# One memory map for three stages of a float32 image kernel: buffers of the next stage filled in the tail of the last, the turn between them in halves, transform rows and five tiles kept in SBUF

## What is computed

```python
xn = layernorm(groupnorm(x))                       # 64 channels
left  = (xn @ left_w  + b) * mask * sigmoid(xn @ lgate_w + b)
right = (xn @ right_w + b) * mask * sigmoid(xn @ rgate_w + b)
out = einsum('bkjd,bkid->bijd', left, right)       # 512x512x512 in each of 64 channels
out = (layernorm(out) @ out_w + out_b) * sigmoid(xn @ ogate_w + b)
x = x + out                                        # layer 0; the result is "x1" below
f = fft2(groupnorm(x))[:12, :12]                   # 12 x 12 modes of each channel
x = x + real(ifft2(f mixed by a complex 64x64 weight in each mode))   # layer 1
```

## Time and profile before

| | |
|---|---|
| device time, median of 3 runs | 3049.51 us (3048.06 to 3056.5) |
| the profiled execution, time | 3050.38 us |
| the profiled execution, span | 3048.6 us |
| mean granted PE clock | 0.950 of full speed |
| PE, DVE, ACT, POOL busy | 83%, 72%, 45%, 33% of the span |
| moved by DMA | 950.26 MB, 312 GB/s over the span |

### The profile page before, as it was taken

How to read it: one execution, slowest core, us unless ns; L and a number is a source line. 1 busy time by engine, 2 the same in 40 slices (tenths; PEclk the granted TensorE clock), 3 DMA queues, 4 the chain that set the end, 5 groups by cost and what they waited for, 6 DMA issues and landing times. The chain is left out here.

```text
span 3048.6 us, 40917 instructions
## 1 busy us (share of the span) xinstructions
PE 2516.1 (83%) x12694; PEld 1875.4 (62%) x12694; DVE 2203.9 (72%) x3463; ACT 1373.3 (45%) x1778; POOL 1021.2 (33%) x1042
## 2 busy tenths in 40 slices
PE   0008999989989979999999993889898899789785
PEld 0005666656666648888888882556565666588664
DVE  5997888778778848898888986667676676326443
ACT  0007888778778866677666672112122122100000
POOL 1018888778778820000000000344444444300000
PEclk9999999999999989999999996899999999769998
DMA  9845888887878766777777773999999999849999
GB/s 375 341 182 203 316 318 313 305 309 287 301 298 297 289 269 254 283 287 276 278 281 282 288 276 103 381 373 382 379 386 366 376 389 374 266 162 382 419 419 406
DMA packets 260650, 950.26 MB, mean 312 GB/s; under 512 B 31153, under 2 KB 31665, under 8 KB 260146
## 3 DMA queue, kind: packets, MB, share of 16 engines
q1 hardware_dynamic: 226160, 877.25, 76.2%
q10 hardware_dynamic: 34370, 71.54, 6.1%
HBM read 540.83 MB, written 407.90 MB: 311 GB/s over the span
## 5 line engine op out<-in xcount | busy, mean ns | idle before, releaser
L652 DVE SCALAR_TENSOR_TENSOR pj_lr<-pj_v_ps,layer_b_val,pj_sig 128x1024 f32<-128x1024 f32 x256 | 328.7, 1284 | 163.2 <-ACT pj_sig L589 162.7
L1104 POOL TENSOR_TENSOR fi_square_sum<-fi_square_sum,fi_square 128x1024 f32<-128x1024 f32 x128 | 302.8, 2366 | 424.7 <-ACT fi_square L1075 424.7
L780 PE MATMUL ct_acc_ps<-ct_l_hi,ct_r_hi 128*128 128x512 f32 x1024 | 406.2, 397 | 20.6 <-ACT ct_l_hi L794 20.6
L781 PE MATMUL ct_acc_ps<-ct_l_lo,ct_r_hi 128*128 128x512 f32 x1024 | 405.9, 396 | 0.0
L782 PE MATMUL ct_acc_ps<-ct_l_hi,ct_r_lo 128*128 128x512 f32 x1024 | 405.9, 396 | 0.0
L1075 ACT ACTIVATE fi_square<-fi_x 128x1024 f32<-128x1024 f32 x128 | 135.4, 1058 | 596.0 <-DVE fi_x L1132 583.9
L490 POOL TENSOR_TENSOR front_ring<-front_ring,layer_gn_shift 128x512 f32<-128x512 f32 x256 | 331.2, 1295 | 40.3 <-DVE front_ring L618 40.3
L1031 PE MATMUL fi_y_ps<-fi_scaled,layer_w_bd 128*128 128x512 f32 x512 | 280.7, 631 | 65.5 <-DVE fi_scaled L1115 65.4
L1115 DVE TENSOR_TENSOR fi_scaled<-fi_m,fi_s_ps 128x512 f32<-128x512 f32 x256 | 174.3, 681 | 191.0 <-DMA fi_m<-mixed_d 166.0
L589 ACT ACTIVATE pj_sig<-pj_g_ps,layer_b_gate 128x1024 f32<-128x1024 f32 x256 | 285.6, 1116 | 42.6 <-PE pj_g_ps L555 37.4
L1302 PE MATMUL la_ps_ps<-la_col,la_inv_cols 128*128 128x256 f32 x1024 | 242.9, 400 | 50.1 <-DVE la_early L1372 28.5
(11 more groups left out here) (183 smaller groups left out, 4979.9 us busy)
## 6 DMA issues: line engine op xcount, KB each, us to landing
lr_d<-pj_lr SPq DMA_DIRECT2D x128, 1024.0 KB, 5.4
gate_d<-pj_gout SPq DMA_DIRECT2D x128, 512.0 KB, 6.8
ct_l<-lr_d SPq DMA_DIRECT2D x64, 1024.0 KB, 7.0
ct_r<-lr_d SPq DMA_DIRECT2D x64, 1024.0 KB, 9.0
mixed_d<-ct_o SPq DMA_DIRECT2D x64, 1024.0 KB, 5.0
fi_m<-mixed_d SPq DMA_DIRECT2D x128, 512.0 KB, 14.2
fi_g<-gate_d SPq DMA_DIRECT2D x128, 512.0 KB, 13.3
fi_x<-in_x SPq DMA_DIRECT2D x32, 2048.0 KB, 9.4
```

Source lines behind the costliest of these rows:

```text
L652: dve.scalar_tensor_tensor(out=out[:, :, RG * (m % 2):RG * (m % 2) + RG], in0=v_ps[:, :].rearrange("p (q i) -> p q i", i=RG), scalar=keep. ...
L780: pe.matmul(bank, high, l_hi[b][:, :, k, :], start=(k == 0), stop=False)
L781: pe.matmul(bank, high, l_lo[b][:, :, k, :], start=False, stop=False)
L1104: pool.tensor_tensor(square_sum[:, :, :], square_sum[:, :, :], square[:, :, :], ALU.add).then_inc(sum_done, 1)
```

## The change

- **One area.** The SBUF tiles of `contract`, `finish_layer0` and `layer1` lie at fixed places of one tile `area` (a new class `Shared`), and the matrices that only the front needs are given back after `project`. So SP can fill buffers of `finish_layer0` during the last channel of `contract`.
- **Filled early.** At the last channel SP issues the loads of four gate chunks and x tiles 0 to 3, then the last store of `mixed_d`, then x tile 4; after the stores of `mixed_d` have landed, four mixed chunks.
- **The turn.** Mean squared is taken on ACT. One multiplication by a mask made beforehand on POOL takes the place of two. From there on the chain works in two halves (e = 0, 1) of 128x1024. The high part goes by four DMAs of a half straight from SBUF to its place in `st` on ACT's queue, the low part on SP's; `scale_d` is gone.
- **`finish_layer0`.** Its slots are written out for SP, ACT, POOL and DVE too (PE's were). The x ring has five tiles. The transform has two PSUM banks. Its four small DMAs go into one SBUF tile `rows` (one partition each, runs of 1 KB) and come ahead of the x1 store; the last five x1 tiles are not stored but stay where they are.
- **`layer1`.** No load of the rows. The ring has eight buffers, five of them hold the kept tiles, which are worked on first; one load comes after the column transform, two after the inverse over the rows, the others as stores free their buffers. Stores to `out` are issued by ACT, loads by SP.

```diff
+class Shared:
+    def __init__(self, t, x, mixed_d, gate_d):
+        self.xt = [self.at("fi", f"x{b}", 16 * b, [TG, WS, C]) for b in range(XT)]      # XT = 5
+        self.mt = [self.at("fi", f"m{b}", 80 + 4 * b, [GW]) for b in range(MB)]         # MB = 4
+        self.gt = [self.at("fi", f"g{b}", 96 + 4 * b, [GW]) for b in range(MB)]
+        self.rows = self.at("fi", "rows", 112, [M2, TG * C])
+        self.st = self.at("fi", "s", 136, [RG, GW], F32R)
...
 def contract(nc, lr_d, mixed_d, keep, mid):
...
+        def spread_part(eng, part, source, e):
+            for q in range(RG):
+                rows = slice(P // 4 * q, P // 4 * q + P // 4)
+                at = P // 2 * part + P // 4 * e
+                eng.dma_start(mid.st[at:at + P // 4, q, :].bitcast(F32),
+                              source[rows, e, :, :].rearrange("p t j -> p (t j)").bitcast(F32)).then_inc(mid.s_loaded, DMA)
...
+                if isinstance(n, int) and n == C - 1:
+                    for c in range(MB):
+                        mid.load_gate(sp, c)
+                    sp.wait_ge(l_low, C)
+                    sp.wait_ge(r_low, C)
+                    for k in range(2):
+                        mid.load_x(sp, k)
+                    sp.wait_ge(summed, WT * (C - 1))
+                    for k in range(2, 4):
+                        mid.load_x(sp, k)
                 sp.wait_ge(out_dve, n + 1)
                 sp.wait_ge(out_act, 3 * n + 3)
                 sp.dma_start(view[2][n], flat(om[b])).then_inc(stored[b], DMA)
 
             channels(sp, body)
-            sp.wait_ge(scale_split, 2)
-            for k in range(2):
-                sp.dma_start(scale_v[k], flat((r_hi, r_lo)[k][0]).bitcast(F32)).then_inc(scale_stored, DMA)
-            sp.wait_ge(scale_stored, 2 * DMA)
+            sp.wait_ge(summed, WT * C)
+            for k in range(4, XT):
+                mid.load_x(sp, k)
             for b in range(2):
                 sp.wait_ge(stored[b], DMA * (C // 2))
+            for c in range(MB):
+                mid.load_mixed(sp, c)
+            for e in range(2):
+                sp.wait_ge(low_ready, e + 1)
+                spread_part(sp, 1, s_low, e)
...
+            act.activation(mean_sq[:, :, :, :], total[:, :, :, :], ACT.Square, scale=1.0 / C).then_inc(mean_squared, 1)
+            for e in range(2):
+                act.wait_ge(root_in, e + 1)
+                act.activation(total_sq[:, e, :, :], total_sq[:, e, :, :], ACT.Sqrt, bias=keep.eps[:, 0:1]).then_inc(root_ready, 1)
+            for e in range(2):
+                act.wait_ge(scale_ready, e + 1)
+                act.activation(s_high[:, e, :, :], total[:, e, :, :], ACT.Copy).then_inc(high_ready, 1)
+                act.wait_ge(high_ready, e + 1)
+                spread_part(act, 0, s_high, e)
...
+            for e in range(2):
+                dve.wait_ge(root_ready, e + 1)
+                link(dve.reciprocal(total[:, e, :, :], total_sq[:, e, :, :]))
+                dve.tensor_tensor(total[:, e, :, :], total[:, e, :, :], keep.mask_row[:, e, :, :],
+                                  ALU.mult).then_inc(scale_ready, 1)
+            for e in range(2):
+                dve.wait_ge(high_ready, e + 1)
+                dve.tensor_tensor(s_low[:, e, :, :], total[:, e, :, :], s_high[:, e, :, :], ALU.subtract).then_inc(low_ready, 1)
...
 def finish_layer0(nc, x1_d, keep, mid):
...
+                k = n // TH + 3
+                if n % TH == 4 and XT <= k < TILES:
+                    sp.wait_ge(x1_stored[k % XT], DMA * (k // XT))
+                    mid.load_x(sp, k)
...
                 if piece == 0:
                     pe.wait_ge(x1_ready, TG * k + TG)
-                    at_least(pe, f_copied, k)
+                    at_least(pe, f_copied, k - 1)
...
-                    act.dma_start(x1_v[k], xt[tile][:, :, :, :].rearrange("p g t c -> p g (t c)")).then_inc(x1_stored[tile], DMA)
                     for r in range(RG):
-                        act.dma_start(f_v[k, r], four[b][M2 * r:M2 * r + M2, :, :]).then_inc(f_stored[b], DMA)
+                        act.dma_start(mid.rows[RG * k + r:RG * k + r + 1, :, :], four[b][M2 * r:M2 * r + M2, :, :]).then_inc(
+                            f_stored[b], DMA)
+                    if k < KEPT:                                                      # 27
+                        act.dma_start(x1_v[k], xt[k % XT].rearrange("p g t c -> p g (t c)")).then_inc(x1_stored[k % XT], DMA)
...
 def layer1(nc, x1_d, w_real, w_imag, inverse_rows, inverse_columns, out, keep, mid):
...
+    XR = XT + 3
+    TILE = [(KEPT + n) % NTG for n in range(NTG)]
...
-            sp.dma_start(early[:, 0:M2 * WT * C], fourier_d.rearrange("p m r c -> p (m r c)")).then_inc(f_loaded, DMA)
...
+            sp.wait_ge(f_ready, 1)
+            load(XT)
+            sp.wait_ge(col_ready, C // CB)
+            for n in range(XT + 1, XR):
+                load(n)
+            for n in range(XR, NTG):
+                sp.wait_ge(stored[n % XR], DMA * (n // XR))
+                load(n)
...
+            for n in range(NTG):
+                act.wait_ge(y_done, WS // 2 * n + WS // 2)
+                act.dma_start(o_v[TILE[n]], by_group(xt[n % XR])).then_inc(stored[n % XR], DMA)
```

More of the change, by code:

```diff
@@ L975, in at_least, with halves, inside @@
+        block = ctx.enter_context(nc.Block())
+        def halves(lead, slot):
+            for n in range(-lead, HALVES + 2 * TH + 4):
+                slot(n)
+        def inside(n, count=HALVES):
+            return 0 <= n < count
         def at_least(eng, sem, value):
-            if not (is_int(value) and value <= 0):
+            if value > 0:
                 eng.wait_ge(sem, value)
-        def part(m, j, ahead, size):
-            return (LOOP // size) * j + (m + ahead) // size
         @block.sync
@@ L1010, in slot @@
                     sp.wait_ge(y_gated, n + 1)
-                    load_gate(c + MR, m // 2 % MR)
-                if m % TH == 4 and ahead_of(n, 2 * TH, HALVES):
-                    k = part(m, j, 2 * TH, TH)
-                    b = (m // TH + 2) % XR
-                    if not (is_int(k) and k < XR):
-                        sp.wait_ge(x1_stored[b], DMA * part(m, j, 2 * TH, LOOP))
-                    load_x(k, b)
-            halves(sp, 0, slot)
+                    mid.load_gate(sp, c)
@@ L1091, in _ @@
+            halves(0, slot)
+            for b in range(XT):
+                act.wait_ge(x1_stored[b], DMA * len(range(b, KEPT, XT)))
             for b in range(2):
-                act.wait_ge(f_stored[b], RG * DMA * (GROUPS // TG // 2))
+                act.wait_ge(f_stored[b], RG * DMA * (TILES // 2))
         @block.gpsimd
@@ L1097, in _, with slot @@
             pool.wait_ge(sum_set, 1)
-            def slot(n, m, j):
-                if m % 2 == 1 and ahead_of(n, -3, HALVES):
-                    g = part(m, j, -3, 2)
+            def slot(n):
+                if n % 2 == 1 and inside(n - 3):
+                    g = n // 2 - 1
                     pool.wait_ge(squared, g + 1)
@@ L1144, in _ @@
+            halves(2, slot)
             link = chained(dve, step)
```

395 lines of the change are left out of this document (184 added, 211 removed).

## The result

| | before | after |
|---|---|---|
| median of the runs, us | 3049.59 (3046.72 to 3056.5, n = 8) | 3065.61 (3059.31 to 3076.67, n = 8) |
| profiled execution: time, span | 3050.4, 3048.6 | 3064.27, 3062.5 |
| ratio of the times | | 1.0055 (1.0042 to 1.0068) |

The kernel became 16 us slower, 0.55%, where 60 us less were forecast. The interval is clear of 1, so the change is real, though small. The parts before and behind `finish_layer0`'s steady loop came out close to the forecast, and the loop took back more than all of them.

A forecast was written before the change was run, and what follows sets the result against it. DMA traffic and its waits were taken to set finish_layer0's pace, with little moving at the turn and layer1's start. 3050.4 - 17.7 - 3.3 - 8 - 17.2 - 14.5 = 2989.7, so 2990 us; range 2955 to 3025.

The forecast's parts named there:

- Step 3: finish_layer0's steady loop, halves 20 to 255: 648.0 us against 652.1, plus 4 for full buffers, 8 us less.
- I take 0.5 us, near the low end: Loop: cost a tile of four small DMAs into neighbouring partitions, between 0.24 and 7.6 us; cancels 0.55 saved.
- That costs nothing while SP's queue still holds loads, as it does then: Loop: small DMAs ahead of the x1 store start it some 1.9 us later, at no cost.
- The order that makes the loop stays: Loop: slot 4 still waits for a store issued two slots earlier, so 22.43 us a tile stays the base.
- another 4: Loop start: full buffers at half 20 give two tiles at 20.7 us before the DMAs are behind, 4 us less.
- Rival B: Loop longer through single-partition row DMAs: over 2.3 us a tile, chance 0.05; 1 to 2.3 us, 3016 to 3050, chance 0.12.
- Step 1: Turn from contract to finish_layer0: 17.7 us less, first matmul of the finish at 1892, bounds 1886 and 1902.
- Step 2: Halves 0 to 20 of finish_layer0: PE sets the pace, 47 us instead of 50.3, 3.3 us less.
- The tail: Last 27 halves of finish_layer0, without x loads or x1 stores: 2.40 us each, 64.8 us.
- Step 4: Last gate to last stage: earlier transform end, 5.8 us, and no reload of rows, 11.6; given as 17.2 us less.
- the tie of PE and weights: Start of layer1: weights there some 25.5 us after the start, PE at 26.1; counted 0, up to 2 more.
- Step 5: Last stage: 297 us instead of 311.5, from the idle start and both waits in one queue, 14.5 us less.

The follow-up runs named there:

- e2: Changed kernel with each row DMA landing in 24 partitions instead of one (rows misplaced, only measures): 23.12 us a tile, 3008.54 us.
- e4: Changed kernel with SP loading the next x tile a tile later: 22.29 us a tile, 2990.28 us.
- g2: Changed kernel with the x load a tile later and the four row DMAs left out (only measures): 20.11 us a tile, 2925.46 us.
- g3: Changed kernel with the x load a tile later, x1 store first, rows to DRAM and one reload at layer1's start: 20.44 us a tile, 2944.73 us.
- e1: Changed kernel with ACT issuing the x1 store ahead of the four row DMAs: 23.49 us a tile, 3019.31 us.
- e3: Changed kernel with the four row DMAs left out and rows zeroed once (only measures): 22.19 us a tile, 2980.33 us.
- g1: Changed kernel with the x1 store first, rows to DRAM and one reload at layer1's start: 22.19 us a tile, 2991.08 us.
- h3: g3 with rows of tiles 0 to 26 reloaded in slot 248, the last five tiles' written directly, x tile 4 loaded behind the factor's low parts: 2937.41 us.

## Why the prediction was wrong

**Step 3 failed, in two of its terms,** and with it the sign; a third passage of it missed a chance.

"I take 0.5 us, near the low end": the four DMAs into neighbouring partitions cost 2.06 us a tile more than the same four with wide targets (e2), 2.18 without SP's wait (e4 against g2). I had both ends, 0.24 and 7.6. The window nearest to the case, 0.86 busy for 177 GB/s, pointed to the slow end, and "98 KB are 1.2% of a tile's traffic" was no reason to leave it. Bytes don't tell what a transfer holds up: in the burst the packets of the other transfers slow down as well (242 ns, against 160 with rows to DRAM in g3), and 5 us pass at some 240 GB/s. The rule of the Trainium skill, "SBUF — State Buffer", section "Door 1: The DMA port swizzle", that I had as a rival, gives the order of the three right: by it the four neighbours reach one port, the rows 32 apart two, the rows 4 apart four. My estimate with it, 3.8 us, took the count of ports from that page and the rate from the weights' window (206 / 8 GB/s); with the page's own rate of about 27 GB/s a port it is an estimate of 3.6 us. Both are above the 2.0 us of transfer that the windows show as lost, and more ports brought less than it would give: twice the ports took 0.33 us off T and four times the ports 1.15.

"That costs nothing while SP's queue still holds loads, as it does then": it did not. ACT's issues took 3.04 us instead of 1.90, the store started later and its data ran beside the slow burst; the DMAs had next to nothing to do from 2226 to 2230. With the store first, 1.69 us a tile come back (e1). The argument looked at how full the queue was in the kernel before, where the small DMAs went to DRAM. The question should have been asked of the new loop.

"The order that makes the loop stays", with 22.43 as base: right as to the order, but I took SP's 273.8 us of waits as given, and said of the fifth buffer that "x was not what was late". This is a chance missed by the change rather than a part of the 16 us. The buffer is what makes the later load possible. With five buffers and the load a tile later, the store that SP waits for was issued ten slots before instead of two. Used so it is worth 2.08 us a tile without rows and 2.89 with them, 54 to 75 us in 26 tiles, as much as all seams together (22.0 + 16.6 + 16.0); the change used it to load earlier. Of the "another 4" us for the full buffers, which I gave to two tiles, one tile shows a gain: the first behind half 20 took 20.6 us, the second 30.4.

The burst and the store kept back together: 25.18 - 22.19 = 2.99 us a tile for 26 tiles is 77.7 us; without row DMAs the changed kernel is at 2980 (e3), 10 from the forecast. So the rest of the sum held as a whole. Part of that is luck, as steps 1 and 2 below show.

**Rival B** was the right place: "It decides from 2.3 us a tile on", and the loop came to 2.75 more. It had 0.05, and the 25.18 us a tile lie outside the range, which ended at B with 1.3. B's price, 3.25 net, was for the burst alone and was near the total partly by luck. By e2 the burst is 2.06 of the 2.99 us that the rows cost; the other 0.93 goes when the four DMAs are left out (e3) or go to DRAM behind the store (g1), which fits a store that is kept back, and it is what carried B over the line. A rival of which only the first half is worked out is weighed too low.

**Step 1** (17.7 less, first matmul at 1892): 1897.92, so 11.8 less. The chain was right: the last low half was done at 1881.9 (1879.47 + 2.43) where I had 1882.7. What failed is the landing. Eight parts into 32 partitions each took 12.6 us in the median, at 216 GB/s with share 1.08 from 1892 to 1896, and my 1892 left them too little time. I had put it down to "what ends last is probably SP's queue"; h3 takes 2 MB out of that queue and gains 0.3 us. It doesn't test what else lies beside them, the high parts and the mixed chunks.

**Step 2** (3.3 less): 9.9 less. "A little less as the first ten have no transform" was mis-sized: a tile's transform is 7.12 us, 0.89 a half, so ten halves save 8.9. 48.0 - 8.9 = 39.1, and the gates show 40.4. That steps 1 and 2 together came to 22.0 where I had 21.0 is luck: 5.9 too much in one, 6.6 too little in the other.

**The tail** in step 3, 64.8 us, was 65.85. **Step 4** (17.2 less, though its two parts, 5.8 and 11.6, add up to 17.4) was 16.6: PE started with the block, and in the tie of PE and weights the weights came last; they landed 26.1 us after issue, and PE waited 3.84 us for them where it had waited 2.79 for DVE, 1.05 us more. **Step 5** (297 us) was 295.5.

## What to carry to other kernels

Don't price a small DMA by its bytes alone. If its target is one partition, or a few neighbouring ones, look in single microseconds at what all the queues move while it runs, and write to DRAM or to many partitions if the GB/s drop at a full share. Before such transfers are put ahead of one for which another queue's issuer waits, work out the new loop, not the old one. When buffers are added to a loop with a wait in it, use them first to take the wait away, by issuing the load later, into a buffer that has long been free.
